# A graph attention layer in split precision: attention by pairs of heads, and low parts of weight slabs on VectorE

## Chip, cores, metric

One core of a Trainium2 chip. The metric is the device time of one execution in microseconds.

## The reference

`x` is 384x1024, H = 16 heads of D = 64, N = 384 nodes, 6528 edges; all weights are 1024x1024, all data float32.

```python
h = maximum(layernorm(x), 0)
q = h @ wq.T + bq;  k = h @ wk.T + bk;  v = h @ wv.T + bv
q2 = (q @ wiq.T + biq);  k2 = (k @ wik.T + bik);  v2 = (v @ wiv.T + biv)   # cut into 16 heads of 64
mask = full((N, N), -inf); mask[src, dst] = softplus(edge_weights)[type - 1]; diagonal filled
scores = q2 @ k2.T / 8 + mask          # per head, 384x384
out = softmax(scores) @ v2             # per head, 384x64
y = x + out @ wo.T + bo
```

## The kernel before

**Split products.** A float32 array is held as a high part rounded to fp32r (`hi`) and the rest (`lo`). A product is three matmuls: hi by hi, lo by hi, hi by lo (`products`, L735, L736, L739). ScalarE writes the high part, VectorE or GpSimd subtracts it from the source.

**Slabs.** The weights come as 56 slabs of 512 KB. SyncE loads slab `s` into `raw` (3 buffers) once the low part of slab `s-3` exists. `split_hi(s)` (ScalarE, L387) fills one of four `w_hi` buffers, `split_lo(s)` fills `w_lo` on VectorE (L629) or GpSimd (L322), as `lo_by_vector` says: before, odd slabs below 16 and all of 16 to 37 by VectorE, the others (0 and the even ones below 16, and 38 to 55) by GpSimd.

**Stages**, each engine running its own instructions in the order written, with waits on semaphores: layernorm and transposes; v (slabs 0 to 7), v2 (8 to 15), q (16 to 23), k (24 to 31); slabs 32 to 47 alternate between q2 and k2, one slab (`tile`, 24 matmuls) for 128 output rows, that is for a pair of heads; slabs 48 to 55 are the output projection (`out_part`, seven pieces, each a sum over 8 row blocks `k`, block `k` being head pair `k`). In the first two stages VectorE also works out each edge's cell (`edge_unit`: four L523, then L532 and L535), and GpSimd scatters the values into `cells` in DRAM (`scatter`); `build_mask` reads them back later. GpSimd adds the bias `bo` to the reloaded x (L367).

**Attention**, loop over heads `i`. A q2/k2 tile is evacuated by `tile_hi_part` and `tile_lo_part` in halves of 64 partitions: for each head, q2 high stands on its own 64 partitions and q2 low on the other 64. `k2_other_half` (VectorE, L617, four copies of 64x384 per pair) puts k2 high and k2 low on both halves. So `scores(i)` needs two matmuls of 128 rows per block of 128 nodes (L850, L852), six per head. Per head then: VectorE adds the mask and takes the row maximum (L688), scales it (L674); ScalarE takes the exponential (L470); VectorE inverts the sum; GpSimd multiplies (L375); one step later TensorE transposes the nine 128x128 blocks (`turn_probs`, L862), ScalarE and VectorE split them (L466, L679), and `heads_values` multiplies by v2 (L877, L878). ScalarE (L482, half of the result plus bias), VectorE (L721) and ScalarE again (L458, `a_hi`), then GpSimd (`a_lo`), put the head's result together. Between the transposes and `heads_values` of a step stands one tile of 24 matmuls, or, in the last steps, part of the output projection.

## Time and profile before

| | us |
|---|---|
| median of 3 runs (lowest, highest) | 330.95 (326.81, 332.99) |
| profiled execution: device time | 330.76 |
| its span, first to last instruction | 329.2 |
| TensorE busy in it | 301.1 (91%) |
| VectorE / ScalarE / GpSimd busy | 221.5 / 163.6 / 169.8 |

The device time holds 1.56 us beside the span. The profile's durations of matmuls overlap, since they are pipelined: the distance between two starts is what one costs. A wait names the instruction whose end released it.

### The profile page before, as it was taken

The page shows a single profiled execution, that of the slowest core. Times are in us where ns is not written, and L with a number is a line of the kernel's source. Part 1 is how long each engine was busy: PE and PEld are TensorE (multiplying, and loading weights), DVE is VectorE, ACT ScalarE, POOL GpSimd, SP SyncE. Part 2 cuts the span into 40 slices and gives each one's busy share as a digit, 9 for nine tenths or more (in the row PEclk, how much of TensorE's full clock was granted, in tenths as well). Part 3 has the DMA queues.
Part 4 walks back from the last instruction along what each step waited for, and adds up shares of the span by engine and source line. Part 5 has one row for each costly group of instructions (what it writes and reads, how often), then busy time and mean ns, then how long its engine had stood idle before and what let it go on. Part 6 is the DMA issues. An engine that isn't in the chain of part 4 may idle for free.

```text
span 329.2 us, 4826 instructions
## 1 busy us (share of the span) xinstructions
PE 301.1 (91%) x1696; PEld 280.2 (85%) x1696; DVE 221.5 (67%) x568; ACT 163.6 (50%) x304; POOL 169.8 (52%) x156
## 2 busy tenths in 40 slices
PE   1879999999999999999969997979797979999996
PEld 0569899788899999999969997979797979878886
DVE  4887986943444444444896979797979796992231
ACT  3663533233433333333445785858586765794300
POOL 5416777765446555555705565655556464456200
PEclk9999999999999999999998999999999998999999
DMA  7816444338733343436332122020212111121031
GB/s 203 343 65 193 126 131 128 130 130 273 286 116 120 126 120 125 129 129 196 127 127 64 67 87 105 10 103 22 85 41 72 58 64 67 64 86 43 2 127 66
DMA packets 13640, 37.48 MB, mean 114 GB/s; under 512 B 3248, under 2 KB 4528, under 8 KB 13616
## 3 DMA queue, kind: packets, MB, share of 16 engines
q1 hardware_dynamic: 11312, 35.93, 32.3%
q0 software_dynamic: 2016, 1.21, 1.5%
q8 instruction: 14, 0.23, 0.3%
q14 instruction: 10, 0.08, 0.1%
q10 hardware_dynamic: 288, 0.03, 0.1%
HBM read 34.38 MB, written 2.78 MB: 113 GB/s over the span
## 4 chain that ended last, share of the span: by engine, by line
PE 62%; DVE 21%; ACT 9%; DMA 3%; issue 3%; SPq 1%; POOL 0%; DVEq 0%
PE bank L735 18%; PE bank L739 18%; PE bank L736 18%; DVE k_lo L617 5%; DVE k_lo L602 3%; ACT prob L470 3%; DVE w_lo L629 3%; PE bank L862 2%; DVE k_hi L617 2%; PE bank L850 2%; ACT pt_hi L466 2%; DMA raw<-in_slabs 2%; DMA x_sb<-in_x 2%; PE bank L852 2%; ACT k_hi L398 1%
## 5 line engine op out<-in xcount | busy, mean ns | idle before, releaser
L349 POOL DMA_INDIRECT cells<-value,cell x51 | 56.0, 1099 | 47.4 <-DMA cells<-value,cell 39.6
L735 PE MATMUL bank<-a_hi,w_hi 128*128 128x384 f32 x192 | 65.3, 340 | 1.5 <-DVE w_lo L629 0.9
L387 ACT ACTIVATE w_hi<-raw 128x1024 fp32r<-128x1024 f32 x51 | 53.5, 1053 | 24.6 <-PE bank L739 18.4
L739 PE MATMUL bank<-a_lo,w_hi 128*128 128x384 f32 x192 | 64.5, 336 | 1.0 <-DVE a_lo L642 1.0
L736 PE MATMUL bank<-a_hi,w_lo 128*128 128x384 f32 x192 | 64.2, 334 | 0.0
L375 POOL TENSOR_SCALAR prob<-prob,row_inv 128x384 f32<-128x384 f32 x42 | 25.8, 628 | 62.4 <-DVE row_inv L703 62.4
L322 POOL TENSOR_TENSOR w_lo<-raw,w_hi 128x1024 fp32r<-128x1024 f32 x21 | 51.0, 2427 | 7.1 <-ACT w_hi L387 6.9
L629 DVE TENSOR_TENSOR w_lo<-raw,w_hi 128x1024 fp32r<-128x1024 f32 x30 | 41.4, 1381 | 15.0 <-ACT w_hi L387 14.5
L735 PEld LDWEIGHTS bank<-a_hi,w_hi 128*128 128x128 f32 x192 | 36.1, 188 | 1.9 <-DVE w_lo L629 1.1
L739 PEld LDWEIGHTS bank<-a_lo,w_hi 128*128 128x128 f32 x192 | 36.0, 188 | 1.7 <-DVE a_lo L642 1.5
L736 PEld LDWEIGHTS bank<-a_hi,w_lo 128*128 128x128 f32 x192 | 36.1, 188 | 0.0
L466 ACT ACTIVATE pt_hi<-bank 128x384 fp32r<-128x384 f32 x48 | 20.1, 488 | 23.4 <-PE bank L862 23.3
L470 ACT ACTIVATE prob<-prob,neg_max 128x384 f32<-128x384 f32 x48 | 29.1, 615 | 5.2 <-DVE neg_max L674 5.2
L850 PE MATMUL bank<-k_hi,q 128*128 128x384 f32 x48 | 18.2, 378 | 13.5 <-DVE k_lo L617 13.5
L679 DVE TENSOR_TENSOR pt_lo<-bank,pt_hi 128x384 fp32r<-128x384 f32 x48 | 23.7, 549 | 3.9 <-ACT pt_hi L466 3.8
L393 ACT ACTIVATE b_hi<-bank,bias 128x384 fp32r<-128x384 f32 x16 | 9.3, 581 | 34.0 <-PE bank L739 34.0
L688 DVE CUSTOM_DVE_ANT_0 prob<-bank,work 128x384 f32<-128x384 f32 x48 | 25.1, 548 | 0.3
L592 DVE SCALAR_TENSOR_TENSOR b_lo<-bank,bias,b_hi 128x384 fp32r<-128x384 f32 x16 | 9.9, 616 | 21.1 <-ACT b_hi L393 21.0
L850 PEld LDWEIGHTS bank<-k_hi,q 128*128 128x128 f32 x48 | 9.7, 203 | 16.1 <-DVE k_lo L617 16.1
L735 PE MATMUL bank<-b_hi,w_hi 128*128 128x384 f32 x64 | 22.0, 343 | 0.5 <-DVE q L602 0.5
L735 PE MATMUL bank<-c_hi,w_hi 128*128 128x384 f32 x64 | 22.3, 349 | 0.0
L736 PE MATMUL bank<-c_hi,w_lo 128*128 128x384 f32 x64 | 21.7, 339 | 0.0
(131 smaller groups left out, 694.9 us busy)
## 6 DMA issues: line engine op xcount, KB each, us to landing
raw<-in_slabs SPq DMA_DIRECT2D x56, 512.0 KB
x_sb<-in_x SPq DMA_DIRECT2D x5, 512.0 KB, 6.1
out_y<-x_sb SPq DMA_DIRECT2D x5, 256.0 KB, 2.2
cells<-prob SPq DMA_DIRECT2D x2, 576.0 KB, 9.7
cells<-value,cell POOLq DMA_INDIRECT x51
work<-cells POOLq DMA_DIRECT2D x1, 576.0 KB, 4.9
prob<-cells POOLq DMA_DIRECT2D x1, 576.0 KB, 6.5
x_sb<-in_x SPq DMA_DIRECT2D x2, 256.0 KB, 3.2
```

The source lines that it names most:

```text
L322: nc.gpsimd.tensor_tensor(lo, raw[:, s % RAW, :], hi.bitcast(F32), ALU.subtract).then_inc(slab_lo, 1)
L349: nc.gpsimd.indirect_dma_start(out=cells[c][:, :], out_offset=bass.IndirectOffsetOnAxis(ap=cell[:, t:t + 1], axis=0), in_=value[:, t:t + 1 ...
L375: nc.gpsimd.tensor_scalar(prob[:, i % 2, t, :], prob[:, i % 2, t, :], row_inv[:, i % 2, t:t + 1], 1.0, ALU.mult, ALU.mult).then_inc(prob_o ...
L387: nc.scalar.activation(split_place(s)[0], raw[:, s % RAW, :], ACT.Copy).then_inc(slab_hi, 1)
L466: nc.scalar.activation(pt_hi[:, m, :], pt_bank[m][:, 0:N], ACT.Copy).then_inc(pt_hi_ok, 1)
L470: nc.scalar.activation(prob[:, i % 2, t, :], prob[:, i % 2, t, :], ACT.Exp, scale=SCALE, bias=neg_max[:, i % 2, t:t + 1], accum_out=row_su ...
L629: nc.vector.tensor_tensor(lo, raw[:, s % RAW, :], hi.bitcast(F32), ALU.subtract).then_inc(slab_lo_dve, 1)
L688: nc.vector.tensor_tensor_reduce(out=prob[:, i % 2, t, :], in0=score_bank[t][:, 0:N], in1=mask[:, t, :], scale=1.0, scalar=-3.4e38, op0=AL ...
L735: nc.tensor.matmul(psum, w[0], a[0], start=first, stop=False)
L736: nc.tensor.matmul(psum, w[1], a[0], start=False, stop=False)
L739: return nc.tensor.matmul(psum, w[0], a[1], start=False, stop=last)
L850: nc.tensor.matmul(score_bank[n][:, 0:N], q2[:, turn, h % 2, m], k2_hi[:, turn, h % 2, :], start=True, stop=False)
```

## The change

The attention loop runs over pairs of heads `j`. q2 and k2 are kept as plain high and low parts of 128 partitions, head `2j` on the first 64 and `2j+1` on the last; `k2_other_half` is gone, and each tile is evacuated by one instruction on each engine in place of two. `scores(j, n)` gives block `n` of both heads by three matmuls each of 64 rows, taken from the two heads in turn and written to two PSUM banks. Four banks serve scores and two the transposes. VectorE takes the minimum of the negated scores, which is the bias of the exponential, so L674 goes. In a step the work of pair `j` (scores, maximum, exponential) is interleaved with the transposes and values of both heads of pair `j-1`, and the slab tiles are cut in two halves of 12 matmuls (`filler`); the output projection is spread over the last three steps in another order, and at the end all seven pieces are closed by their last block in turn. VectorE adds `bo` to x during pair 0, where GpSimd did it before. VectorE makes the low parts of slabs 1 to 37. GpSimd keeps slab 0 and slabs 38 to 55, and the multiplications of all blocks.

TensorE where the scores of a new pair begin, before (`q2` and `k2_hi`, `k2_lo` are the operands, bank 0 to 2 the scores, bank 5 the transposed probabilities):

```order
L850 MATMUL bank0<-k2_hi,q2 128x384 [waits masked,tile_lo]
L852 MATMUL bank0<-k2_lo,q2 128x384
L850 MATMUL bank1<-k2_hi,q2 128x384 [waits masked]
L852 MATMUL bank1<-k2_lo,q2 128x384
L850 MATMUL bank2<-k2_hi,q2 128x384 [waits masked]
L852 MATMUL bank2<-k2_lo,q2 128x384
L862 MATMUL bank5<-ident,prob 128x128 [waits pt_lo_ok,prob_ok]
L862 MATMUL bank5<-ident,prob 128x128 x2
```

and now:

```order
L880 MATMUL bank0<-k2_hi,q2_hi 128x384 [waits masked,tile_lo]
L880 MATMUL bank1<-k2_hi,q2_hi 128x384
L880 MATMUL bank0<-k2_lo,q2_hi 128x384
L880 MATMUL bank1<-k2_lo,q2_hi 128x384
L880 MATMUL bank0<-k2_hi,q2_lo 128x384
L880 MATMUL bank1<-k2_hi,q2_lo 128x384
L880 MATMUL bank2<-k2_hi,q2_hi 128x384
L880 MATMUL bank7<-k2_hi,q2_hi 128x384
L880 MATMUL bank2<-k2_lo,q2_hi 128x384
L880 MATMUL bank7<-k2_lo,q2_hi 128x384
L880 MATMUL bank2<-k2_hi,q2_lo 128x384
L880 MATMUL bank7<-k2_hi,q2_lo 128x384
```

The scores of the pair's first two blocks are twelve 64-row matmuls, in twos on the two halves of the partitions, with the wait at the first; the transposes follow behind these.

VectorE between the first head's and the second head's work, before, from the split of the transposed probabilities on:

```order
L679 TENSOR_TENSOR pt_lo<-bank,pt_hi 128x384 [waits pt_hi_ok] x3
L703 RECIPROCAL row_inv<-row_sum 128x1 [waits exp_done] x3
L617 CAST k_hi<-k_hi 64x384 [waits k2_read,k2_step]
L617 CAST k_hi<-k_hi 64x384
L617 CAST k_lo<-k_lo 64x384 x2
L602 SCALAR_TENSOR_TENSOR q<-bank,bias,q 64x384 [waits tile_hi] x2
L721 TENSOR_TENSOR work<-bank,work 64x384 [waits head_lo,half_ok]
```

and now, over the start of a pair:

```order
L695 TENSOR_TENSOR pt_lo<-bank,pt_hi 128x384 [waits pt_hi_ok] x2
L691 RECIPROCAL row_inv<-row_sum 128x1 [waits exp_done] x2
L695 TENSOR_TENSOR pt_lo<-bank,pt_hi 128x384 [waits pt_hi_ok]
L618 SCALAR_TENSOR_TENSOR q_lo<-bank,bias,q_hi 128x384 [waits tile_hi]
L681 ISA prob,neg_max<-bank,work 128x384 [waits score_done]
L681 ISA neg_max 128x1
L681 ISA work,neg_max<-bank,work 128x384 [waits score_done]
L681 ISA neg_max 128x1
L704 TENSOR_TENSOR work<-bank,work 64x384 [waits head_lo,half_ok]
```

The four copies in front of the next scores are gone, and the result of the last head stands between the two parts of the maximum.

VectorE in the first step of attention, before, with the maximum of head 0:

```order
L688 ISA prob,row_max<-bank,work 128x384 [waits mask_ok,score_done]
L688 ISA row_max 128x1
L688 ISA prob,row_max<-bank,work 128x384 [waits mask_ok,score_done]
L688 ISA row_max 128x1
L674 TENSOR_SCALAR neg_max<-row_max 128x1 [waits masked]
L688 ISA prob,row_max<-bank,work 128x384 [waits mask_ok,score_done]
L688 ISA row_max 128x1
L674 TENSOR_SCALAR neg_max<-row_max 128x1 [waits masked] x2
L703 RECIPROCAL row_inv<-row_sum 128x1 [waits exp_done] x3
```

and now, from the fourth block of the maximum of pair 0:

```order
L681 ISA prob,neg_max<-bank,work 128x384 [waits score_done]
L681 ISA neg_max 128x1
L710 TENSOR_TENSOR x_sb<-x_sb,work 128x1024 [waits y_in]
L691 RECIPROCAL row_inv<-row_sum 128x1 [waits exp_done] x2
L710 TENSOR_TENSOR x_sb<-x_sb,work 128x1024 [waits y_in]
L691 RECIPROCAL row_inv<-row_sum 128x1 [waits exp_done] x2
L710 TENSOR_TENSOR x_sb<-x_sb,work 128x1024 [waits y_in]
L618 SCALAR_TENSOR_TENSOR k_lo<-bank,bias,k_hi 128x384 [waits tile_hi]
```

The additions of `bo` stand between the maxima and the inversions.

```diff
-        q2 = sb("q2", [P, 2, 2, N], F32R)
-        k2_hi = sb("k2_hi", [P, 2, 2, N], F32R)
-        k2_lo = sb("k2_lo", [P, 2, 2, N], F32R)
+        q2_hi = sb("q2_hi", [P, 2, N], F32R)
+        q2_lo = sb("q2_lo", [P, 2, N], F32R)
+        k2_hi = sb("k2_hi", [P, 2, N], F32R)
+        k2_lo = sb("k2_lo", [P, 2, N], F32R)
         work = sb("work", [P, NT * N + N], F32)
-        prob = sb("prob", [P, 2, NT, N], F32)
+        prob = sb("prob", [P, 3, NT, N], F32)
...
+        probs = [[prob[:, 0], prob[:, 1]],
+                 [prob[:, 2], work2[:, 0:NT * N].rearrange("p (t n) -> p t n", n=N)]]
...
-        score_bank = bank[0:3]
-        pt_bank = bank[5:8]
+        score_bank = [bank[0], bank[1], bank[2], bank[7]]
+        pt_bank = bank[5:7]
...
-            return s % 2 == 1 if s < LO_SHARED else s < LO_ALL
+            return 1 <= s < LO_ALL
...
+        def slabs_of_step(j):
+            return [range(38 + 2 * j, 39 + 2 * j), range(39 + 2 * j, 40 + 2 * j)] if j < PAIRS - 2 else [
+                range(50 + 3 * (j - 6), 51 + 3 * (j - 6)), range(51 + 3 * (j - 6), 53 + 3 * (j - 6))]
...
-            for s in range(2, LO_SHARED, 2):
-                split_lo(s)
...
-            pool.wait_ge(y_in, 16 * (NT + 1))
-            for t in range(NT):
-                nc.gpsimd.tensor_tensor(y[:, t, :], y[:, t, :], bo_sb, ALU.add).then_inc(y_ok, 1)
...
+            def norm_part(j, n):
+                for x in range(2):
+                    c = 2 * n + x
+                    pool.wait_ge(inv_ok, chunk_at(j, n, x) + 1)
+                    nc.gpsimd.tensor_scalar(probs[j % 2][x][:, n, :], probs[j % 2][x][:, n, :],
+                                            row_inv[:, j % 2, c:c + 1], 1.0, ALU.mult, ALU.mult).then_inc(prob_ok, 1)
+            for j in range(PAIRS):
+                first, second = slabs_of_step(j)
+                norm_part(j, 0)
+                norm_part(j, 1)
+                if j >= 2:
+                    pair_lo_part(j - 2)
+                for s in first:
+                    split_lo(s)
+                norm_part(j, 2)
+                for s in second:
                     split_lo(s)
...
+            for j in range(PAIRS + 1):
+                first, second = slabs_of_step(j) if j < PAIRS else ((), ())
+                h = 2 * (j - 1)
+                if j >= 2:
+                    half_part(h - 1)
+                if j < PAIRS:
+                    exp_part(j, 0)
+                if j >= 2:
+                    pair_hi_part(j - 2)
+                if j >= 1:
+                    pt_hi_part(h, 0)
+                    pt_hi_part(h, 1)
+                if j < PAIRS:
+                    exp_part(j, 1)
+                for s in first:
                     split_hi(s)
...
+                if j >= 1:
+                    pt_hi_part(h, 2)
+                if j < PAIRS - 1:
+                    tile_hi_part(3 * KT + 3 + 2 * j)
+                if j < PAIRS:
+                    exp_part(j, 2)
+                if j >= 1:
+                    half_part(h)
+                    pt_hi_part(h + 1, 0)
+                    pt_hi_part(h + 1, 1)
+                for s in second:
+                    split_hi(s)
+                if j >= 1:
+                    pt_hi_part(h + 1, 2)
+                if j < PAIRS - 2:
+                    tile_hi_part(3 * KT + 4 + 2 * j)
+            half_part(H - 1)
...
-            def k2_other_half(pair):
...
-            split_lo(1)
+            for s in range(1, AHEAD):
+                split_lo(s)
...
-                    if s == QK0 + 1:
-                        k2_other_half(0)
...
+            def max_part(j, n):
+                for x in range(2):
+                    c, at = 2 * n + x, chunk_at(j, n, x)
+                    dve.wait_ge(score_done, at + 1)
+                    if at == 0:
+                        dve.wait_ge(mask_ok, 1)
+                    if at == 6:
+                        dve.wait_ge(y_ok, NT)
+                    nc.vector.tensor_tensor_reduce(
+                        out=probs[j % 2][x][:, n, :], in0=score_bank[c % 4][:, 0:N], in1=mask[:, n, :], scale=-SCALE,
+                        scalar=3.4e38, op0=ALU.add, op1=ALU.min,
+                        accum_out=neg_max[:, j % 2, c:c + 1]).then_inc(masked, 1)
...
+            def y_part(t):
+                dve.wait_ge(y_in, 16 * (NT + 1))
+                nc.vector.tensor_tensor(y[:, t, :], y[:, t, :], bo_sb, ALU.add).then_inc(y_ok, 1)
+            for j in range(PAIRS + 1):
+                h = 2 * (j - 1)
+                if j < PAIRS:
+                    max_part(j, 0)
+                if j >= 2:
+                    head_part(h - 1)
+                if j < PAIRS:
+                    max_part(j, 1)
+                    if j == 0:
+                        y_part(0)
+                    inv_part(j, 0)
+                    if j == 0:
+                        y_part(1)
+                if j == PAIRS:
                     pair_lo_part(PAIRS - 2)
...
+                if j >= 1:
+                    pt_lo_part(h, 0)
+                    pt_lo_part(h, 1)
+                if j < PAIRS:
+                    inv_part(j, 1)
+                    if j == 0:
+                        y_part(2)
+                if j >= 1:
+                    pt_lo_part(h, 2)
+                if j < PAIRS - 1:
+                    tile_lo_part(3 * KT + 3 + 2 * j)
+                if j < PAIRS:
+                    max_part(j, 2)
+                if j >= 1:
+                    head_part(h)
+                    pt_lo_part(h + 1, 0)
+                    pt_lo_part(h + 1, 1)
+                if j < PAIRS:
+                    inv_part(j, 2)
+                if j >= 1:
+                    pt_lo_part(h + 1, 2)
+                if j < PAIRS - 2:
+                    tile_lo_part(3 * KT + 4 + 2 * j)
+            head_part(H - 1)
...
-            def scores(h):
-                turn = h // 2 % 2
-                if h % 2 == 0:
-                    pe.wait_ge(tile_lo, 3 * KT + h + 2)
+                    tile(t, c_hi, c_lo, ks)
+            def scores(j, n):
+                turn, m = j % 2, slice(n * P, (n + 1) * P)
+                if n == 0:
+                    pe.wait_ge(tile_lo, 3 * KT + 2 * j + 2)
+                for x in range(2):
+                    at = chunk_at(j, n, x)
+                    if n == 0 and j >= 1:
+                        pe.wait_ge(masked, at - 1)
+                    elif n == NT - 1:
+                        pe.wait_ge(masked, at - 3)
+                for p, (q, k) in enumerate(((q2_hi, k2_hi), (q2_hi, k2_lo), (q2_lo, k2_hi))):
+                    for x in range(2):
+                        own, _ = rows_of(x)
+                        mm = nc.tensor.matmul(score_bank[(2 * n + x) % 4][:, 0:N], q[own, turn, m], k[own, turn, :],
+                                              start=(p == 0), stop=(p == 2))
+                        if p == 2:
+                            mm.then_inc(score_done, 1)
+            def turn_probs(h, m):
+                i = h * NT + m
+                if m == 0:
+                    pe.wait_ge(prob_ok, chunk_at(h // 2, NT - 1, h % 2) + 1)
+                if i >= 2:
+                    pe.wait_ge(pt_lo_ok, i - 1)
                 for n in range(NT):
-                    if h >= 1:
-                        pe.wait_ge(masked, (h - 1) * NT + n + 1)
-                    m = slice(n * P, (n + 1) * P)
-                    nc.tensor.matmul(score_bank[n][:, 0:N], q2[:, turn, h % 2, m], k2_hi[:, turn, h % 2, :],
-                                     start=True, stop=False)
-                    nc.tensor.matmul(score_bank[n][:, 0:N], q2[:, turn, h % 2, m], k2_lo[:, turn, h % 2, :],
-                                     start=False, stop=True).then_inc(score_done, 1)
-            def turn_probs(h):
-                pe.wait_ge(prob_ok, (h + 1) * NT)
-                for m in range(NT):
-                    if h >= 1:
-                        pe.wait_ge(pt_lo_ok, (h - 1) * NT + m + 1)
-                    for n in range(NT):
-                        mm = nc.tensor.transpose(pt_bank[m][:, n * P:(n + 1) * P],
-                                                 prob[:, h % 2, n, m * P:(m + 1) * P], ident[:])
-                    mm.then_inc(pt_done, 1)
+                    mm = nc.tensor.transpose(pt_bank[i % 2][:, n * P:(n + 1) * P],
+                                             probs[h // 2 % 2][h % 2][:, n, m * P:(m + 1) * P], ident[:])
+                mm.then_inc(pt_done, 1)
...
+            halves = (range(0, KT // 2), range(KT // 2, KT))
+            def filler(j, at):
+                if j < PAIRS - 1 and at < 2:
+                    pair_tile(3 * KT + 3 + 2 * j, halves[at])
+                elif j < PAIRS - 2:
+                    pair_tile(3 * KT + 4 + 2 * j, halves[at - 2])
+                elif j == PAIRS - 2:
+                    if at == 2:
+                        pe.wait_ge(tile_lo, 5 * KT)
+                    out_part(0, range(2 * (at - 2), 2 * (at - 2) + 2))
+                elif j == PAIRS - 1:
+                    if at == 0:
+                        out_part(0, range(4, 5))
+                    elif at == 1:
+                        pe.wait_ge(masked, chunk_at(j, 1, 0) + 1)
+                        out_part(1, range(0, 5))
+                    elif at == 2:
+                        out_part(0, range(5, 6))
+                        pe.wait_ge(masked, chunk_at(j, 2, 0) + 1)
+                        out_part(2, range(0, 3))
+                    else:
+                        out_part(2, range(3, 6))
+                        out_part(1, range(5, 6))
+                elif at == 0:
+                    out_part(3, range(0, 3))
+                elif at == 1:
+                    out_part(3, range(3, 6))
+                elif at == 2:
+                    out_part(4, range(0, 4))
                 else:
+                    out_part(4, range(4, 6))
                     for n in range(NT):
                         out_part(n, [KT - 2])
...
-                    heads_values(i - 1)
-            out_part(NT, range(0, KT - 1))
-            for n in range(NT):
-                out_part(n, [KT - 1])
-            out_part(NT, [KT - 1])
-            out_part(NT + 1, range(KT))
-            out_part(NT + 2, range(KT))
-            out_part(NT + 3, range(KT))
+            for j in range(PAIRS + 1):
+                h = 2 * (j - 1)
+                if j < PAIRS:
+                    scores(j, 0)
+                    scores(j, 1)
+                if j >= 1:
+                    turn_probs(h, 0)
+                    turn_probs(h, 1)
+                filler(j, 0)
+                if j >= 1:
+                    turn_probs(h, 2)
+                filler(j, 1)
+                if j < PAIRS:
+                    scores(j, 2)
+                if j >= 1:
+                    heads_values(h)
+                    turn_probs(h + 1, 0)
+                    turn_probs(h + 1, 1)
+                filler(j, 2)
+                if j >= 1:
+                    turn_probs(h + 1, 2)
+                filler(j, 3)
+                if j >= 1:
+                    heads_values(h + 1)
+            for piece in (3, 4):
+                out_part(piece, [KT - 2])
+            out_part(NT + 2, range(0, KT - 1))
+            out_part(NT + 3, range(0, KT - 1))
+            for piece in range(len(out_pieces)):
+                out_part(piece, [KT - 1])
```

## Rows read from the trace of the kernel before

**Rows 1.** The page: the chain that ended last, by line.

```profile
PE bank L735 18%; PE bank L739 18%; PE bank L736 18%; DVE k_lo L617 5%; DVE k_lo L602 3%; ACT prob L470 3%; DVE w_lo L629 3%; PE bank L862 2%; DVE k_hi L617 2%; PE bank L850 2%; ACT pt_hi L466 2%; DMA raw<-in_slabs 2%; DMA x_sb<-in_x 2%; PE bank L852 2%; ACT k_hi L398 1%
```

**Rows 2.** Waits of TensorE: who for whom, total, times, longest.

```profile
PE bank L850 <- DVE k_lo L617: 13.5, 8, 2.3
```

**Rows 3.** Windows: stretch, length, busy PE, PEld, DVE, ACT, POOL, clock, DMA.

```profile
171.84:186.10 14.26, 14.26 (x75) 13.96 (x75) 11.11 (x36) 9.05 (x21) 6.07 (x7) 0.88 0.22 74
237.16:254.04 16.88, 14.77 (x91) 14.38 (x91) 14.41 (x41) 11.90 (x27) 9.44 (x9) 1.00 0.18 62
270.90:286.10 15.20, 14.92 (x78) 13.97 (x78) 11.80 (x38) 10.46 (x25) 5.19 (x5) 0.89 0.22 71
```

**Rows 4.** Timeline, VectorE and GpSimd between two pairs of heads.

```profile
234.03 3.08 DVE L617 CAST k_lo<-k_lo 64x384 fp32r<-64x384 f32 x2
...
234.44 2.45 POOL L322 TENSOR_TENSOR w_lo<-raw,w_hi 128x1024 fp32r<-128x1024 f32 x1
```

**Rows 5.** Timeline of TensorE after that: start, duration.

```profile
237.16 0.44 PE L850 MATMUL bank<-k_hi,q 128*128 128x384 f32 x1 [2.12 <-DVE k_lo L617]
...
238.32 1.14 PE L862 MATMUL bank<-ident,prob 128*128 128x128 f32 x9
239.22 0.42 PE L735 MATMUL bank<-c_hi,w_hi 128*128 128x384 f32 x1
239.48 0.34 PE L736 MATMUL bank<-c_hi,w_lo 128*128 128x384 f32 x1
...
243.32 0.33 PE L739 MATMUL bank<-c_lo,w_hi 128*128 128x384 f32 x1
```

**Rows 6.** Timeline around the start of attention, three engines.

```profile
155.53 7.10 POOL L367 TENSOR_TENSOR x_sb<-x_sb,work 128x1024 f32<-128x1024 f32 x3
...
157.96 5.76 DVE L629 TENSOR_TENSOR w_lo<-raw,w_hi 128x1024 fp32r<-128x1024 f32 x1 [0.33 <-ACT w_hi L387]
...
165.15 0.41 PE L735 MATMUL bank<-b_hi,w_hi 128*128 128x384 f32 x1 [0.46 <-DVE q L602]
...
171.84 0.66 PE L850 MATMUL bank<-k_hi,q 128*128 128x384 f32 x1 [2.29 <-DVE k_lo L617]
...
175.17 0.41 PE L736 MATMUL bank<-c_hi,w_lo 128*128 128x384 f32 x1
```

**Rows 7.** Timeline of the value projection, tiles 3 and 4.

```profile
33.13 3.03 DVE L532 SCALAR_TENSOR_TENSOR live<-later,key_dump 128x4 f32<-128x4 f32 x1
...
33.71 2.42 POOL L322 TENSOR_TENSOR w_lo<-raw,w_hi 128x1024 fp32r<-128x1024 f32 x1
...
38.23 0.41 PE L735 MATMUL bank<-a_hi,w_hi 128*128 128x384 f32 x1 [0.53 <-DVE b_lo L592]
```

**Rows 8.** The page: groups of instructions, busy, mean ns of one.

```profile
L375 POOL TENSOR_SCALAR prob<-prob,row_inv 128x384 f32<-128x384 f32 x42 | 25.8, 628 | 62.4 <-DVE row_inv L703 62.4
L322 POOL TENSOR_TENSOR w_lo<-raw,w_hi 128x1024 fp32r<-128x1024 f32 x21 | 51.0, 2427 | 7.1 <-ACT w_hi L387 6.9
...
L466 ACT ACTIVATE pt_hi<-bank 128x384 fp32r<-128x384 f32 x48 | 20.1, 488 | 23.4 <-PE bank L862 23.3
L470 ACT ACTIVATE prob<-prob,neg_max 128x384 f32<-128x384 f32 x48 | 29.1, 615 | 5.2 <-DVE neg_max L674 5.2
...
L679 DVE TENSOR_TENSOR pt_lo<-bank,pt_hi 128x384 fp32r<-128x384 f32 x48 | 23.7, 549 | 3.9 <-ACT pt_hi L466 3.8
...
L688 DVE CUSTOM_DVE_ANT_0 prob<-bank,work 128x384 f32<-128x384 f32 x48 | 25.1, 548 | 0.3
```

**Rows 9.** Timeline of TensorE, the last output pieces.

```profile
320.09 0.39 PE L739 MATMUL bank<-c_lo,a_hi 128*128 128x512 f32 x1
320.32 0.28 PE L735 MATMUL bank<-b_hi,a_hi 128*128 128x256 f32 x1
...
325.95 0.28 PE L739 MATMUL bank<-c_lo,a_hi 128*128 128x256 f32 x1
```

**Rows 10.** The page: issues of the output's DMA.

```profile
out_y<-x_sb SPq DMA_DIRECT2D x5, 256.0 KB, 2.2
```

214 lines of the change are left out of this document (54 added, 160 removed).

## The prediction

> **What bounds the kernel now.** I read the chain that ended last first. Matmuls of the slab tiles (L735, L736, L739) carry 54% of it, and the next names are VectorE's low parts and copies of k2, L617 and L602 [rows 1]. So the end is set by TensorE, and by what it waits for. The waits of TensorE say for what: 13.5 us in eight waits of the scores for L617 [rows 2]. The windows give the loop: a pair of heads takes 16.88 us, in which the other engines have room [rows 3].
>
> Then the cost of each kind of TensorE work, by distances between starts [rows 5]. A tile's 2nd matmul starts at 239.48 and its 24th at 243.32: 0.174 us each. Nine transposes go from 238.32 to 239.22, 0.10 each. The first matmul behind them takes 0.26 to the next start, 0.09 more than usual. A pair is 48 tile matmuls (8.35), 12 of scores (2.09), 12 of values (2.09), 18 transposes with two such seams (1.98): 14.5 us. The other 2.4 us of the 16.88 is the wait of 2.12 and its restart.
>
> The wait has a cause of its own: the two copies of k2 low take 3.08 us, beside GpSimd's slab subtraction from 234.44 to 236.89 [rows 4]. The same picture stands twice elsewhere. A subtraction on four elements takes VectorE 3.03 us while GpSimd subtracts a slab from 33.71 to 36.13 [rows 7]. One slab's low part takes 5.76 us from 157.96, and GpSimd's additions of `bo` end at 162.63, 1.1 us before it [rows 6]. VectorE's instructions with all operands in SBUF stand still while GpSimd works; by the last case such a low part costs 1.1 us when alone.
>
> **The sum, against the profiled execution** (span 329.2, device time 330.76, 0.19 below the median; I add the 1.56 us beside the span at the end).
>
> *Low parts of slabs 2 to 14 to VectorE.* TensorE's only wait here that they can touch is 0.53 us at 38.23, for a tile's low part that stood behind the 3.03 us [rows 7]. Per two tiles (8.4 us) VectorE takes on 1.1 us and loses a block of up to 3.0, so I count the wait and its restart as gone: -0.6. If VectorE were late by all it takes on, it would be +7.7 (7 x 1.1). Edge cells come up to 1.1 us later each; GpSimd, rid of seven times 2.43 us [rows 8], scatters earlier, behind the matmuls of five stages: the mask is read only at the entry into attention. SyncE, which loads slab s after the low part of s-3, gets the even ones sooner: nothing.
>
> *Entry into attention.* Without GpSimd's additions the 5.76 us become 1.1, and without `k2_other_half(0)` the scores follow the tile from 165.15 at once: it starts 0.55 earlier (0.46 and restart) and ends 24 x 0.174 = 4.2 later, at 169.3 by the old clock of the trace, against scores at 171.84 [rows 6]. That is -3.1.
>
> *Clock.* After that wait the granted clock is at the 1.2 GHz level: ten starts take 3.33 us (171.84 to 175.17) instead of 1.74, 1.6 lost [rows 6]; the window's mean is 0.88, and the window from 270.90 has 0.89, the same loss again [rows 3]. Both follow an idle TensorE of over 2 us; none that long is left: -3.2. The other waits of about 2.1 us kept 2.4 GHz (1.00 in the window of 237.16), so a return of the drop is possible without a warning.
>
> *The copies.* Seven waits besides the first hold 13.5 - 2.3 = 11.2 us; with restarts (2.4 for 2.12) 12.7: -12.7. The halved evacuations, L674 and the copies leave VectorE with slack in every step; worth nothing by itself.
>
> *Scores.* 96 matmuls of 128 rows (16.7 us) become 144 of 64 rows. No row shows a 64-row matmul. Upper bound: each costs 0.174, whatever its rows, 25.1 us. Lower bound: two on different halves of the partitions and in different banks cost as one, 72 x 0.174 = 12.5. Each still loads its own 128 columns of weights, and transposes, which also load for each matmul, come every 0.10 [rows 5]; two loads are 0.20. I take 72 x 0.20 = 14.4, because that row holds the nearest limit if the halves work side by side: -2.3. (By the Trainium skill, TensorE: Matmul & The Clock Gate, Part 3, small matmuls at different row positions run at once, a pack costing one duration and some 4 ns for each more; the sum would then be 1.6 us lower than mine. No row here shows it.)
>
> *Seams.* Transposes come in four groups per pair instead of two (16 more seams in all) and scores in two groups with a seam at either end (32): 48 x 0.09 = +4.3 [rows 5]. Bounds for the 32: nothing, or a drained array. A matmul lasts 0.33 and its successor starts after 0.17; waiting for its end and restarting (0.44 against 0.33 for the first after a wait) is 0.16 + 0.11 = 0.27, which makes +5.8 more.
>
> *New waits.* In a step, the transposes of block 2 wait for the low part of block 0, as two banks serve them. By [rows 5, 8], from the first score matmul: scores of block 0 are out at 0.9 with what lies between engines; two maxima to 2.0 (0.55 each); two exponentials to 2.7 (0.6); `a_hi` 3.2; `pt_hi` of block 0 3.7; VectorE, after head result, maxima and inversions at 3.8, has `pt_lo` at 4.3. TensorE is there at 4.1 (scores 1.3, six transposes 0.7, half a tile 2.1). For the second head the same walk gives 11.7 against 11.5. I take 0.5 a step, steps 1 to 5: 2.5. Steps 6 to 8 have shorter fillers, of 512-column matmuls at 0.23 [rows 9]: step 7 starts with three of them (0.7 instead of 2.1), +1.6; step 6, +1.2; step 8, +0.5. Entry of step 1: VectorE's three additions (1.1 each) meet GpSimd's multiplications (0.63) and its slab of 2.43 [rows 8] and wait for them; the maximum of block 2 ends near 10.0, GpSimd then has slab 38 in front, and the multiplied block comes 1.4 after TensorE wants it. Together +7.2; bounds nothing and twice that. Behind TensorE's waiting transposes stands the whole rest of its queue, and GpSimd's, VectorE's and ScalarE's next steps with it.
>
> *Tail.* Last start 325.95, span's end 3.25 us later. Now seven pieces close within 4 us and VectorE and the output DMA (2.2 us a piece [rows 10]) follow in a row: +1.2, between 0 and 3. The matmuls are the same.
>
> Sum: -0.6 - 3.1 - 3.2 - 12.7 - 2.3 + 4.3 + 7.2 + 1.2 = **-9.2**, a span of 320.0 and **321.6 us**.
>
> **Rivals.** (1) *The halves take turns* (slower). Place: L880. Each 64-row matmul costs what a 128-row one does, 0.174: +10.7, 332.3 us, above before. It decides from 0.32 us for two, (330.95 - 321.6)/72 above my 0.20. For it: all TensorE rows show one matmul after another. Against it: they all use all rows. Chance 0.10; with (2) also true, 338, chance 0.02.
>
> (2) *Each change between 128-row and 64-row work drains the array*: 32 x 0.27 instead of 0.09, 327.4 us, chance 0.15. The seam of 0.09 behind the transposes, also a change of kind, speaks against it, no row on a change of rows for it. The Trainium skill, TensorEngine Tiling (Array Packing), Key Properties, has this rule: changing the tiling mode drains TensorE.
>
> (3) *The chain over three engines takes the wait's place*: ScalarE does its exponentials before `pt_hi`, so if each step's two waits come to 1.7 instead of 0.5, all eight steps give 9.6: 331 us. For it: my margins are 0.2 us. Against: the walk counts whole durations, and instructions on one engine follow each other a little faster. Chance 0.08.
>
> (4) *Seams of scores cost nothing and the new waits half*: -2.9 - 3.6, 315.1 us. Chance 0.17. That the copies' wait stays is out: nothing copies any more.
>
> **How the numbers follow.** The forecast, with its own range 318 to 325.5, has 0.48. The range for 8 in 10 reaches from (4)'s 315, with 0.5 for error, to 330.5, with (2) and the lower half of (3) in it: 314.5 to 330.5. Outside lie (1) and a part of (3) and (4). 2% is about what a measurement of this kernel can tell: 324.3 and 337.6. Faster: (4) 0.17, of the forecast 0.43, of (2) and (3) 0.04, 0.64. Slower: 0.03. The same: 0.33.
>
> **What the changed profile would show.** No L617. TensorE's start of scores at about 168.2, and 1.00 clock there. L880 in twos with 0.20 between the twos; 0.174 between single ones is rival 1. The first matmul behind scores 0.26 to its successor; 0.44 is rival 2. A pair at 15.3 us; waits of the transposes for `pt_lo` of 0.2 to 0.3 each, over 0.8 is rival 3. VectorE's L710 longer than 1.1 us beside L369. No wait near 38 us. Wrong I would be most through L880, or a wait that I did not walk to, above all in steps 6 to 8 and in the slabs of the output projection, whose low parts GpSimd still makes.

## The result, and the profile after

| | before | after |
|---|---|---|
| median (lowest, highest), us | 330.73 (326.81, 332.99), 4 runs | 318.87 (318.79, 318.88), 4 runs |
| ratio, 95% interval | | 0.9677 [0.9634, 0.972] |
| profiled span | 329.2 | 317.3 |
| granted clock, mean | 0.989 | 1.00 |

The change makes the kernel 3.2% faster; 321.6 us was forecast, and the range of 314.5 to 330.5 holds the result. Some executions of the kernel before and of three experiments, all with GpSimd making low parts of the first slabs, took 5 us or more longer than the rest, for a reason that isn't shown: the ratios leave them out, the medians given below don't.

The changed kernel's page, busy times, the clock in 40 slices, and the chain that ended last by line, to be read against [rows 1]:

```profile
PE 299.7 (94%) x1744; PEld 270.1 (85%) x1744; DVE 179.1 (56%) x476; ACT 154.7 (49%) x288; POOL 147.0 (46%) x152
...
PEclk9999999999999999999999999999999999999999
...
PE bank L767 23%; PE bank L763 22%; PE bank L764 22%; PE bank L893 4%; PE bank L880 3%; DMA x_sb<-in_x 2%; PE bank L908 2%; ACT prob L461 2%; PE bank L909 2%; DVE work L704 1%; DVE pt_lo L695 1%; ACT work L475 1%; DVE prob L681 1%; DVE x_sb L755 1%; ACT k_hi L395 1%
```

The matmuls of slab tiles (now L763, L764, L767) rose from 54% of the chain to 67%. VectorE's copies are gone from it, its evacuations of k2 are no longer among the lines named, and VectorE is busy 42 us less. The waits of TensorE, in place of [rows 2]:

```profile
PE bank L893 <- DVE pt_lo L695: 2.6, 4, 1.4
```

The windows of the eight steps, from one first score matmul to the next, in the columns of [rows 3]:

```profile
168.21:178.93 10.72, 10.72 (x69) 9.71 (x68) 8.25 (x23) 6.89 (x16) 6.16 (x5) 1.00 0.14 45
178.93:194.22 15.29, 15.14 (x97) 13.52 (x96) 8.63 (x28) 10.43 (x24) 11.55 (x12) 1.00 0.32 104
...
224.82:240.13 15.31, 15.16 (x97) 13.52 (x96) 8.94 (x29) 10.83 (x25) 9.10 (x10) 1.00 0.21 69
...
255.44:270.32 14.88, 14.01 (x86) 11.51 (x85) 8.61 (x28) 11.18 (x25) 8.67 (x10) 1.00 0.22 73
270.32:287.88 17.56, 16.20 (x91) 13.20 (x91) 7.79 (x26) 10.60 (x24) 13.21 (x12) 1.00 0.18 61
```

Scores start at 168.21 in place of 171.84, a pair takes 15.3 us in place of 16.88, and no window is under 1.00. The timeline of TensorE at one start of a step, to be read against [rows 5] (a row joins instructions of one form; x2 are the two heads):

```profile
224.82 0.44 PE L880 MATMUL bank<-k_hi,q_hi 64*128 64x384 f32 x2
225.11 0.34 PE L880 MATMUL bank<-k_lo,q_hi 64*128 64x384 f32 x2
225.28 0.34 PE L880 MATMUL bank<-k_hi,q_lo 64*128 64x384 f32 x2
...
225.80 0.36 PE L880 MATMUL bank<-k_hi,q_lo 64*128 64x384 f32 x2
226.09 0.88 PE L893 MATMUL bank<-ident,prob 128*128 128x128 f32 x6
226.72 0.42 PE L763 MATMUL bank<-c_hi,w_hi 128*128 128x384 f32 x1
...
228.72 0.34 PE L767 MATMUL bank<-c_lo,w_hi 128*128 128x384 f32 x1
229.01 0.55 PE L893 MATMUL bank<-ident,prob 128*128 128x128 f32 x3
229.31 0.42 PE L763 MATMUL bank<-c_hi,w_hi 128*128 128x384 f32 x1
...
231.31 0.34 PE L767 MATMUL bank<-c_lo,w_hi 128*128 128x384 f32 x1
231.58 0.44 PE L880 MATMUL bank<-k_hi,q_hi 64*128 64x384 f32 x2
231.86 0.34 PE L880 MATMUL bank<-k_lo,q_hi 64*128 64x384 f32 x2
232.03 0.34 PE L880 MATMUL bank<-k_hi,q_lo 64*128 64x384 f32 x2
232.30 0.44 PE L908 MATMUL bank<-pt_hi,v 128*128 128x384 f32 x1
232.58 0.34 PE L909 MATMUL bank<-pt_lo,v 128*128 128x384 f32 x1
...
236.02 0.34 PE L767 MATMUL bank<-b_lo,w_hi 128*128 128x384 f32 x1
236.51 0.55 PE L893 MATMUL bank<-ident,work 128*128 128x128 f32 x3 [0.15 <-DVE pt_lo L695]
236.81 0.42 PE L763 MATMUL bank<-b_hi,w_hi 128*128 128x384 f32 x1
```

Three things are to be seen. Two 64-row matmuls take 0.17 together, what one of 128 rows takes. A change of rows lengthens two distances, the one across it and the next: around the scores of block 2 they are 0.27 and 0.28 (231.31 to 231.86) going in and 0.27 and 0.28 (232.03 to 232.58) going out, where 0.17 would be usual, so some 0.2 in all for each change. And the transposes of block 2 come 0.29 and 0.49 behind a tile's last matmul: short waits, of which only one carries a mark. The long ones are in steps 6 to 8:

```profile
267.11 0.55 PE L893 MATMUL bank<-ident,work 128*128 128x128 f32 x3 [0.84 <-DVE pt_lo L695]
...
274.51 0.55 PE L893 MATMUL bank<-ident,prob 128*128 128x128 f32 x3 [1.36 <-DVE pt_lo L695]
...
291.04 0.55 PE L893 MATMUL bank<-ident,prob 128*128 128x128 f32 x3 [0.27 <-DVE pt_lo L695]
```

### The profile page after: what moved, and what is told of

It is laid out like the page before. It is cut to its first block, busy times and chain, and to the rows that moved or that the text cites. A ratio compares the mean times of both kernels' runs of the same rounds, so it can differ in the third digit from the quotient of the medians.

```text
span 317.3 us, 4822 instructions
## 1 busy us (share of the span) xinstructions
PE 299.7 (94%) x1744; PEld 270.1 (85%) x1744; DVE 179.1 (56%) x476; ACT 154.7 (49%) x288; POOL 147.0 (46%) x152
## 4 chain that ended last, share of the span: by engine, by line
PE 79%; DVE 9%; ACT 5%; issue 3%; DMA 2%; SPq 1%; POOL 0%; DVEq 0%; ACTq 0%
PE bank L767 23%; PE bank L763 22%; PE bank L764 22%; PE bank L893 4%; PE bank L880 3%; DMA x_sb<-in_x 2%; PE bank L908 2%; ACT prob L461 2%; PE bank L909 2%; DVE work L704 1%; DVE pt_lo L695 1%; ACT work L475 1%; DVE prob L681 1%; DVE x_sb L755 1%; ACT k_hi L395 1%
## 5 line engine op out<-in xcount | busy, mean ns | idle before, releaser
L763 PE MATMUL bank<-a_hi,w_hi 128*128 128x384 f32 x192 | 65.3, 340 | 0.9 <-DVE w_lo L630 0.9
L767 PE MATMUL bank<-a_lo,w_hi 128*128 128x384 f32 x192 | 64.5, 336 | 1.1 <-DVE a_lo L643 1.0
L764 PE MATMUL bank<-a_hi,w_lo 128*128 128x384 f32 x192 | 64.2, 334 | 0.0
L630 DVE TENSOR_TENSOR w_lo<-raw,w_hi 128x1024 fp32r<-128x1024 f32 x37 | 45.3, 1225 | 18.3 <-ACT w_hi L390 16.2
L369 POOL TENSOR_SCALAR prob<-prob,row_inv 128x384 f32<-128x384 f32 x36 | 22.6, 637 | 69.5 <-DVE row_inv L691 69.5
L767 PEld LDWEIGHTS bank<-a_lo,w_hi 128*128 128x128 f32 x192 | 36.0, 188 | 1.8 <-DVE a_lo L643 1.7
L763 PEld LDWEIGHTS bank<-a_hi,w_hi 128*128 128x128 f32 x192 | 36.1, 188 | 1.4 <-DVE w_lo L630 1.1
L764 PEld LDWEIGHTS bank<-a_hi,w_lo 128*128 128x128 f32 x192 | 36.1, 188 | 0.0
L695 DVE TENSOR_TENSOR pt_lo<-bank,pt_hi 128x384 fp32r<-128x384 f32 x48 | 25.2, 552 | 17.0 <-ACT pt_hi L468 17.0
L325 POOL TENSOR_TENSOR w_lo<-raw,w_hi 128x1024 fp32r<-128x1024 f32 x14 | 33.5, 2392 | 0.0
L461 ACT ACTIVATE prob<-prob,neg_max 128x384 f32<-128x384 f32 x36 | 21.9, 610 | 18.7 <-DVE neg_max L681 18.7
L468 ACT ACTIVATE pt_hi<-bank 128x384 fp32r<-128x384 f32 x48 | 21.5, 482 | 3.5 <-PE bank L893 3.3
L763 PE MATMUL bank<-c_hi,w_hi 128*128 128x384 f32 x64 | 22.5, 352 | 0.0
L681 DVE CUSTOM_DVE_ANT_0 prob<-bank,work 128x384 f32<-128x384 f32 x36 | 18.9, 553 | 6.2 <-PE bank L880 6.0
L763 PE MATMUL bank<-b_hi,w_hi 128*128 128x384 f32 x64 | 22.4, 350 | 0.0
L767 PE MATMUL bank<-b_lo,w_hi 128*128 128x384 f32 x64 | 21.5, 336 | 0.0
L767 PE MATMUL bank<-c_lo,w_hi 128*128 128x384 f32 x64 | 21.5, 336 | 0.0
L764 PE MATMUL bank<-c_hi,w_lo 128*128 128x384 f32 x64 | 21.4, 335 | 0.0
```

The source lines that it names most:

```text
L325: nc.gpsimd.tensor_tensor(lo, raw[:, s % RAW, :], hi.bitcast(F32), ALU.subtract).then_inc(slab_lo, 1)
L369: nc.gpsimd.tensor_scalar(probs[j % 2][x][:, n, :], probs[j % 2][x][:, n, :], row_inv[:, j % 2, c:c + 1], 1.0, ALU.mult, ALU.mult).then_in ...
L461: nc.scalar.activation(probs[j % 2][x][:, n, :], probs[j % 2][x][:, n, :], ACT.Exp, scale=-1.0, bias=neg_max[:, j % 2, c:c + 1], accum_out ...
L468: nc.scalar.activation(pt_hi[:, m, :], pt_bank[(h * NT + m) % 2][:, 0:N], ACT.Copy).then_inc(pt_hi_ok, 1)
L630: nc.vector.tensor_tensor(lo, raw[:, s % RAW, :], hi.bitcast(F32), ALU.subtract).then_inc(slab_lo_dve, 1)
L681: nc.vector.tensor_tensor_reduce(out=probs[j % 2][x][:, n, :], in0=score_bank[c % 4][:, 0:N], in1=mask[:, n, :], scale=-SCALE, scalar=3.4e ...
```

## The experiments

Lines of code in them are those of the kernel that they change.

### Do the halves of the array work side by side?

First, one head's three matmuls ahead of the other's:

```diff
-                for p, (q, k) in enumerate(((q2_hi, k2_hi), (q2_hi, k2_lo), (q2_lo, k2_hi))):
-                    for x in range(2):
+                for x in range(2):
+                    for p, (q, k) in enumerate(((q2_hi, k2_hi), (q2_hi, k2_lo), (q2_lo, k2_hi))):
```

> The changed kernel, with one difference: in each block the three score matmuls of one head come first and those of the other head after them, in place of turns. The count, the shapes, the banks and the seams to 128-row work stay. Theory (two 64-row matmuls cost as one because they stand on different halves of the partitions and overlap): within a head they can't, so 144 matmuls cost up to 0.174 each, 25.1 us in place of the 12.5 that the changed kernel shows; about +12 us, less at most 2.6 for waits on the low parts of the probabilities that this hides: 328 to 332 us, and distances of 0.17 within a head. Rival (a 64-row matmul costs half of a 128-row one by itself, in any order): 318.9 us as now, distances of 0.087.

Measured: 318.97 us (318.76 to 319.24), the changed kernel's 318.87. The first theory forecast 328 to 332 and fell, as it was put; but its timeline does not speak for the rival either:

```profile
224.99 0.45 PE L879 MATMUL bank<-k_hi,q_hi 64*128 64x384 f32 x2
225.27 0.34 PE L879 MATMUL bank<-k_lo,q_hi 64*128 64x384 f32 x2
```

In the program a hi-hi matmul (high part of q2, high part of k2) of head 0 is followed by two more of head 0, and only then comes the second head's hi-hi. In the trace the hi-hi of both heads come together, x2 at 224.99, then both hi-lo. The second head's matmul started beside one that stands three places ahead of it. So the order didn't test what I meant it to: the halves do not wait for each other in program order, over three instructions at least. The next run puts both heads on one half:

```diff
-                        own, _ = rows_of(x)
+                        own, _ = rows_of(0)
```

> The changed kernel, with the score matmuls of both heads on the first 64 partitions (the second head's scores are left out, the first head's are made twice). Count, shape, banks, order and seams stay. The run with one head's three matmuls ahead of the other's cost the same as the changed kernel, and its trace had the twos as before, the matmuls of the second head starting beside those of the first although they stand behind them in the program: so either each half of the array runs its own queue, or a 64-row matmul is cheap by itself. First theory (own queues): on one half nothing runs side by side, 72 more distances of 0.17, +12.5 less up to 2.6 of hidden waits: 329 to 331.5 us, L880 singly every 0.17. Rival (half the rows, half the price): 318.9 us, as now.

Measured: 327.03 us (326.86 to 327.13), span 325.3, 8.0 more than the changed kernel's.

```profile
229.09 0.61 PE L880 MATMUL bank<-k_hi,q_hi 64*128 64x384 f32 x2
229.55 0.51 PE L880 MATMUL bank<-k_lo,q_hi 64*128 64x384 f32 x2
229.90 0.50 PE L880 MATMUL bank<-k_hi,q_lo 64*128 64x384 f32 x2
230.24 0.51 PE L880 MATMUL bank<-k_hi,q_hi 64*128 64x384 f32 x2
```

Twos now come every 0.35, one matmul every 0.17. A 64-row matmul is not cheap by itself; the two halves work side by side, which this shows. That it costs 8.0 and not 12.5 has its reason in the same trace: from step to step it takes 16.31 in place of 15.31, though the scores of a pair take 1.54 more (2.29 against 1.27 up to the transposes, 1.24 against 0.72 for block 2). The other 0.54 are waits for `pt_lo` that are gone: its block-2 transposes follow 0.18 behind the tile, not 0.29 and 0.49, and each group of three takes 0.24, not 0.30. So the changed kernel waits about 0.5 us in each ordinary step.

### What does a change of rows cost?

```diff
                 if j < PAIRS:
                     scores(j, 0)
-                    scores(j, 1)
                 if j >= 1:
                     turn_probs(h, 0)
+                if j < PAIRS:
+                    scores(j, 1)
+                if j >= 1:
                     turn_probs(h, 1)
```

> The changed kernel, with the transposes of block 0 put between the scores of block 0 and those of block 1, in steps 1 to 7: 14 more changes between 64-row and 128-row work, nothing else more. Theory (a change costs about 0.2 us, as the distances 0.26 to 0.29 beside the usual 0.10 and 0.17 show): +2.9, about 321.8 us. Rival a (a change costs what I forecast, 0.09): +1.3, 320.2. Rival b (the array is drained and restarted, 0.27 each): +3.8, 322.7. Since block 0 is transposed 0.8 us earlier, up to 1 us of the waits in steps 6 to 8 may go as well, if they hang on the transposes; I think they hang on ScalarE, which is late there, and stay.

Measured: 320.23 us (320.09 to 320.45), +1.4.

```profile
225.61 0.44 PE L880 MATMUL bank<-k_hi,q_hi 64*128 64x384 f32 x2
...
227.84 0.42 PE L763 MATMUL bank<-c_hi,w_hi 128*128 128x384 f32 x1
...
229.85 0.34 PE L767 MATMUL bank<-c_lo,w_hi 128*128 128x384 f32 x1
230.03 0.49 PE L893 MATMUL bank<-ident,prob 128*128 128x128 f32 x3
```

From the first score matmul to the first tile matmul it takes 2.23 (225.61 to 227.84) where the changed kernel takes 1.90 (224.82 to 226.72): 0.33 for two changes, 0.17 each, in which the six transposes are also cut into two groups of three. For 14 changes that would be 2.3. The missing part is waits without a mark that got shorter: block 2's transposes now stand 0.18 behind the tile and not 0.29, and take 0.24 and not 0.30. So an ordinary step grows by 0.17 only, and the marked waits of TensorE for `pt_lo` gave back 0.4 (2.2 against 2.6). With the 0.2 that the distances in the changed kernel show, a change costs 0.17 to 0.2: neither my 0.09 nor the 0.27 of a drained array.

### Where the gain is: the copies of k2

```diff
-                        last = nc.vector.tensor_copy(part[other, turn, h, :], part[own, turn, h, :].bitcast(F32))
+                        c = slice(0, N) if pair < 2 else slice(0, 1)
+                        last = nc.vector.tensor_copy(part[other, turn, h, c], part[own, turn, h, c].bitcast(F32))
```

> The kernel before; its copies of k2 to the other half of the partitions move one column in place of 384 for pairs 2 to 7 (the copying of the other columns is left out, so scores of these pairs use wrong values there). Theory (the copies' wait of about 1.9 us a pair, with 0.25 for the restart, and the second drop of the clock carry the gain of the change): six waits of 11.2/7 = 1.6 with 0.2 of restart each, -10.8, and the clock's -1.6: about 318 us, that is all the gain of the whole change, though the score matmuls keep their 128 rows. Rival (behind the copies stand other things just as late, VectorE's evacuation of the k2 tile above all): -5 or less, 326 or more.

Measured: 316.49 us (314.16 to 323.26), ratio 0.9597 [0.9419, 0.9774]; the profiled span is 312.9 at clock 1.00. The kernel before has 326.0 at that clock (329.2 less two drops of 1.6), 13.1 more. But 1.8 of this lie ahead of the first scores (170.09 against 171.84 in [rows 6]), where this edit changes nothing:

```profile
152.09 7.12 POOL L367 TENSOR_TENSOR x_sb<-x_sb,work 128x1024 f32<-128x1024 f32 x3
...
153.85 6.46 DVE L630 TENSOR_TENSOR w_lo<-raw,w_hi 128x1024 fp32r<-128x1024 f32 x1 [0.33 <-ACT w_hi L387]
...
170.09 0.45 PE L851 MATMUL bank<-k_hi,q 128*128 128x384 f32 x1 [0.54 <-DVE k_lo L618]
```

GpSimd's additions of `bo` started 3.4 us earlier here than in the profiled execution of the kernel before, and met the slab ahead of the one that they met there. The instructions up to this point are the same in both kernels, so this isn't the edit's work; I take it for the chance of an execution, of which no second trace was taken. The copies' time is worth the other 11.3. Without it the old loop is 4.4 us shorter in span than the changed kernel. So the rest of the new loop costs, and the question is why the copies were late. In the kernel before the two copies of k2 high take 1.12 and the two of k2 low 3.08 [rows 4]; VectorE stands still beside GpSimd.

```profile
232.90 1.12 DVE L617 CAST k_hi<-k_hi 64x384 fp32r<-64x384 f32 x2
```

If that is the cause, it is enough to move them to a place where GpSimd is idle:

```diff
+                if i % 2 == 1 and i < H - TILES_AHEAD:
+                    k2_other_half((i + 1) // 2)
                 if i == H - TILES_AHEAD:
                     k2_other_half(PAIRS - 1)
                 if i < H:
                     for t in range(NT):
                         dve.wait_ge(exp_done, i * NT + t + 1)
                         nc.vector.reciprocal(row_inv[:, i % 2, t:t + 1], row_sum[:, i % 2, t:t + 1]).then_inc(inv_ok, 1)
...
-                if i % 2 == 1 and i < H - TILES_AHEAD:
-                    k2_other_half((i + 1) // 2)
```

> The kernel before, with VectorE's four copies of k2 for the next pair placed ahead of the three inversions of the odd head in place of behind them; nothing else. There GpSimd has nothing to do, because its multiplications wait for the inversions. Theory (the copies are late because GpSimd's slab subtraction holds VectorE off, 3.08 us for two, and not because of their number): the copies take 1.6 to 2.2 us in all in place of 4.2 and end about 3 us earlier, the waits of 1.9 us for pairs 1 to 7 go and with them all drops of the clock but the first: -13 to -14, 316 to 318 us, as good as the changed kernel or better, with scores of 128 rows. Rival (the inversions, 1.6 to 2.2 us later, delay GpSimd's multiplications and the transposes behind them): the wait moves to the transposes, 322 to 329 us.

Measured: 316.56 us (314.74 to 324.96), ratio 0.9523 [0.9411, 0.9635], span 313.7 at clock 1.00. Its timeline of VectorE and GpSimd:

```profile
237.32 1.03 POOL L326 TENSOR_TENSOR a_lo<-work,a_hi 128x384 fp32r<-128x384 f32 x1 [0.60 <-ACT a_hi L458]
...
239.91 0.72 DVE L617 CAST k_hi<-k_hi 64x384 fp32r<-64x384 f32 x2
240.65 0.72 DVE L617 CAST k_lo<-k_lo 64x384 fp32r<-64x384 f32 x2
241.40 0.28 DVE L705 RECIPROCAL row_inv<-row_sum 128x1 f32<-128x1 f32 x3
...
241.67 1.72 POOL L375 TENSOR_SCALAR prob<-prob,row_inv 128x384 f32<-128x384 f32 x3 [3.32 <-DVE row_inv L705]
```

The same four copies take 1.44 us, 0.36 each, less even than expected, because GpSimd does nothing from 238.35 to 241.67. Counted from the head's result ahead of them (L721, at 228.63 before and at 236.12 here) they end 3.2 us earlier: 2.8 of it is their shorter time, 0.5 their earlier place. The waits of TensorE for L617 are 1.0 in three, where [rows 2] has 13.5 in eight. One wait of 0.7 for GpSimd's multiplications is all that came in their place in the attention. The scores start at 170.04 here, again with the same code ahead of them as before, so of the 12.3 us between the two spans at equal clock (326.0 to 313.7) 10.5 are the edit's. So it was the meeting with GpSimd, not the number of copies.

### The low parts alone

```diff
-            return s % 2 == 1 if s < LO_SHARED else s < LO_ALL
+            return 1 <= s < LO_ALL
```

With it go GpSimd's and VectorE's calls of `split_lo`, as in the change.

> The kernel before, with VectorE making the low parts of slabs 1 to 37, and nothing else of the change. Theory (the block of VectorE behind GpSimd's slab subtraction is gone, TensorE waited for it 0.53 us at one place): -0.6, about 330.1 us. Rival (VectorE, with 1.1 us more every second slab, comes late): up to +7.7, with waits of TensorE for the low parts of slabs or tiles below 130 us of the span. Second rival: the edge cells come later by so much that the scattering of the mask reaches the entry into attention: +1 or more, seen as a wait for the mask there.

Measured: 327.78 us (325.57 to 329.12, 10 runs), ratio 0.995 [0.9906, 0.9994]. The profiled span is 324.0 at clock 1.00. The wait near 38 us is gone, as forecast, but the span gained more: its scores start at 168.72, not at 171.84. GpSimd's timeline says why:

```profile
142.41 7.10 POOL L362 TENSOR_TENSOR x_sb<-x_sb,work 128x1024 f32<-128x1024 f32 x3
```

These are its additions of `bo`, 13.1 us earlier than in [rows 6], far more than the 3.4 by which one execution differed from another. Rid of seven slabs it scatters earlier and comes to them earlier, so they don't meet VectorE's last slab ahead of the attention: that takes 1.23 there, not 5.76.

The ten runs also show the clock, because this kernel sits on its edge. Spans by granted clock:

| granted clock | spans, us |
|---|---|
| 1.00 | 324.0, 324.3, 324.3 |
| 0.994, 0.995 | 325.6, 325.8, 326.3 |
| 0.989 | 327.1, 327.1, 327.4, 327.6 |

Each 0.005 of the mean is one drop, of about 1.6 us. So with the same waits of about 2 us in it, this kernel has none, one or two drops from one execution to the next. The kernel before spreads wider still (326.81 to 332.99), and the changed one, with no wait over 1.4 in the attention, has no drop (318.79 to 318.88).

### The low parts shared again, and the bias on either engine

In the changed kernel, the low parts of even slabs below 16 go back to GpSimd:

```diff
-            return 1 <= s < LO_ALL
+            return s % 2 == 1 if s < Q0 else s < LO_ALL
```

> The changed kernel with its second part undone: GpSimd makes the low parts of the even slabs 2 to 14 again. Theory: the wait near 38 us is back, +0.6, about 319.5 us; the attention is not touched. Rival: nothing measurable, 318.9, if the wait of 0.5 is taken up again by a later one; second rival: the shorter work of VectorE lets something else start earlier, below 318.5.

Measured: 318.80 and 319.62 us in the two executions that the ratio counts, 0.9626 [0.9558, 0.9693]; the median of all six is 324.92, the highest 326.60. The profiled run is the one of 318.80, with a span of 317.3, the changed kernel's. So `lo_by_vector`'s new rule is worth between nothing and 0.8 us on top of the rest of the change; VectorE's 3.06 us beside GpSimd's slab are back at 32.52, and TensorE doesn't wait there.

In the changed kernel, `y_part` goes and GpSimd has its loop back:

```diff
+            pool.wait_ge(y_in, 16 * (NT + 1))
+            for t in range(NT):
+                nc.gpsimd.tensor_tensor(y[:, t, :], y[:, t, :], bo_sb, ALU.add).then_inc(y_ok, 1)
```

> The changed kernel with the bias added to x by GpSimd ahead of the attention, as before, and not by VectorE in pair 0. Theory (VectorE's slab subtraction next to the attention takes 5.8 us in place of 1.2 beside GpSimd's additions, and the last tiles wait for it): the entry comes 0.5 to 3 us later, and if TensorE then idles over 2 us the clock drops as it did before, 1.6 more: 319.4 to 323.5 us, with the scores of the first pair starting later than 168.7. Rival (without the copies of k2 the low part of that slab is early enough in any case): 318.9 or less, because VectorE's three additions, and GpSimd's multiplications that stand still beside them, are gone from pair 0.

Measured: 319.02 us (318.59 to 319.55); scores start at 168.07. The theory falls. GpSimd's three additions take from 142.31 to 149.42, again ahead of the place in question, and what they meet is another slab of VectorE:

```profile
140.62 1.23 DVE L634 TENSOR_TENSOR w_lo<-raw,w_hi 128x1024 fp32r<-128x1024 f32 x1 [0.33 <-ACT w_hi L394]
144.78 5.73 DVE L634 TENSOR_TENSOR w_lo<-raw,w_hi 128x1024 fp32r<-128x1024 f32 x1 [0.33 <-ACT w_hi L394]
```

The same 5.7 us as at the entry, but here the slab is not due yet, and nobody waits.

In the kernel before, that loop goes, and VectorE has in its first three heads:

```diff
+                if i < 3:
+                    dve.wait_ge(y_in, 16 * (NT + 1))
+                    nc.vector.tensor_tensor(y[:, i, :], y[:, i, :], bo_sb, ALU.add).then_inc(y_ok, 1)
```

> The kernel before, with the bias added to x by VectorE during the first three heads in place of GpSimd ahead of them, and nothing else of the change. Theory: the slab subtraction of 5.76 us becomes 1.2, the tile behind it starts up to 0.5 us earlier, and the copies of k2 for the first pair, which also ran late, come earlier; whether the clock's first drop goes hangs on whether the wait at the first scores, 2.3 us, shrinks below 2: -0.5 to -3.0, 328 to 330.3 us. Rival: the additions of VectorE fall beside GpSimd's multiplications and slab subtraction in the first heads and cost there what they save: no change.

Measured: 332.37 us (329.09 to 333.24), ratio 1.0007 [0.9949, 1.0065], no change. The slab ahead of the attention takes 1.22 (157.98) and the wait of the first scores falls from 2.29 to 0.40, both as expected, and the next pair gives it back, as its copies stand behind the second addition of `bo` and take 4.35 beside GpSimd (182.22 to 186.59):

```profile
169.26 0.45 PE L850 MATMUL bank<-k_hi,q 128*128 128x384 f32 x1 [0.40 <-DVE k_lo L614]
...
186.64 0.69 PE L850 MATMUL bank<-k_hi,q 128*128 128x384 f32 x1 [3.52 <-DVE k_lo L614]
```

The rival had it: the additions cost later on VectorE what they save ahead. In the changed kernel this edit pays no more than here, as the run before this one shows; it only does no harm.

### The order in the last steps

In steps 6 to 8 ScalarE and VectorE split the transposed probabilities ahead of the exponentials, head results and inversions. The core of it, on ScalarE:

```diff
-                if j < PAIRS:
+                if j < PAIRS - 2:
                     exp_part(j, 0)
...
                     pt_hi_part(h, 1)
+                if j >= PAIRS - 2:
+                    if j < PAIRS:
+                        exp_part(j, 0)
+                    pair_hi_part(j - 2)
```

> The changed kernel with another order of ScalarE and VectorE in the last three steps: the high and low parts of the transposed probabilities come ahead of the exponentials, of the head's result and of the inversions, and the last slab's high part of a step behind them. Theory (the four waits of TensorE for pt_lo, 1.36, 0.84, 0.27 and 0.15 us, 2.6 in all, come from ScalarE's order and not from the transposes): steps 6 to 8 lose their waits, with restarts of 0.1 each -2.8, about 316.1 us; the step of 15.3 us is not touched. Rival (the exponentials, now later, delay GpSimd's multiplications and so the next step's transposes): the waits move to the start of the next step, 318.9 or more.

Measured: 317.44 us (317.18 to 317.67), span 315.8, 1.5 less than the changed kernel. The four marked waits are gone, and two others came:

```profile
269.08 0.44 PE L930 MATMUL bank<-pt_hi,v 128*128 128x384 f32 x1 [0.69 <-DVE pt_lo L707]
273.78 0.50 PE L785 MATMUL bank<-w_hi,a_hi 128*128 128x512 f32 x1 [0.64 <-DVE neg_max L693]
```

So the waits came from the order on ScalarE and VectorE, as the theory said; about half of the 2.8 us expected was lost to what now stood later.

### A version that beats both

The kernel before with early copies, and VectorE making the low parts of slabs 1 to 37:

> The same as the run with early copies, and VectorE makes the low parts of slabs 1 to 37 as in the changed kernel. Theory: the two add up, since they stand in different stages; with the low parts alone the profiled span was 324.0 at a granted clock of 1.00, against 326.0 for the kernel before with its two drops of 1.6 taken off, -2.0: 314 to 316 us, below both kernels. Rival (the first stages' gain is taken up by the wait of the first pair for its copies): 316 to 318, as with early copies alone.

Measured: **314.06 us** (313.79 to 314.71, 4 runs), ratio to before 0.9469 [0.9394, 0.9544]; 1.5% below the changed kernel. Its span is 312.6 at clock 1.00, and its scores start at 168.99. The waits of its TensorE for the copies, and then the timeline at two starts of a pair:

```profile
PE bank L846 <- DVE k_lo L612: 0.9, 3, 0.4
```

```profile
212.23 0.33 PE L846 MATMUL bank<-k_hi,q 128*128 128x384 f32 x1
...
226.78 0.33 PE L846 MATMUL bank<-k_hi,q 128*128 128x384 f32 x1
```

A pair takes 14.55 us. That is the 14.5 that the prediction counted as the work of a pair without the wait, and 0.75 less than in the changed kernel, which saves 0.5 at the scores and pays 0.5 of waits, four changes of rows and two more groups of transposes for it.

## Why the prediction came out as it did

The forecast was the likeliest case; none of the rivals came, though a change of rows cost 0.2, between the 0.09 of the forecast and the 0.27 of rival 2. By its steps, on the span (-9.2 forecast, -11.9 measured):

- *Low parts*, -0.6: the wait near 38 us went, but the step missed the larger effect. "GpSimd, rid of seven times 2.43 us, scatters earlier" stood there, and I stopped at the mask. I didn't follow GpSimd's queue on to the additions of `bo`, which this moves by 13 us.
- *Entry into attention*, -3.1: the scores start 3.6 earlier, which is this term and the 0.5 of the one before, right in size. That a meeting of VectorE's slab with GpSimd's additions made the entry late is borne out, but the cure as I put it, "without GpSimd's additions", isn't needed: with them still on GpSimd the entry is as early (168.07). Either edit alone cures it (168.72 and 169.26); the low parts are enough. And 1.8 of the 3.6 is what the profiled execution of the kernel before was later than others with the same code up to there (170.09 and 170.04 in two runs), which I took for a fixed cost.
- *Clock*, -3.2: right for the execution that it was read from; two drops of 1.6, shown by the spans at each level of the clock.
- *The copies*, -12.7: right within about 1 us. The run with one column shows 11.3, and has a wait of 1.2 for its full copies of pair 1 where the kernel before has 0.39. The runs add what the sum left out, that the gain needed none of the new loop.
- *Scores*, -2.3: the mechanism was right, shown by both heads on one half. The term was mis-sized: twos cost 0.174, the lower bound, not the 0.20 that I took from the transposes; 72 x 0.174 = 12.5, -4.2. Here the rule of the Trainium skill, TensorE: Matmul & The Clock Gate, Part 3, was the better price, and the trace agrees: the twos cost what one 128-row matmul does. And the transposes, from which my 0.20 came, are themselves at 0.08 in groups of three (0.24 from 234.20 to 234.44 in the run on one half), for 16 groups some -1.0 in all, which I didn't forecast.
- *Seams*, +4.3: mis-sized the other way. 32 changes at 0.17 to 0.2, with 16 seams of 0.09, make +6.9 to +7.8. The seam behind transposes was the wrong row to take a change of rows from. The rule of the Trainium skill, TensorEngine Tiling (Array Packing), Key Properties, that a change of mode drains the array, points the right way; the price is below the 0.27 that I made of it. That cancels what the scores gave: nine twos and four changes of a pair come to some 2.3 us, against 2.09 before.
- *New waits*, +7.2: about +6. In steps 1 to 5 the 0.5 each is right (0.54). In steps 6 to 8 the waits of 0.84, 1.36, 0.27 and smaller ones make some 3. The 1.4 at the entry of step 1 did not come: VectorE's additions took 1.2, 1.2 and 1.5, not blocked; it was GpSimd that stood, its four multiplications taking 4.17 in place of 2.3, and it was just in time.
- *Tail*, +1.2: +0.8 (last start 313.26, span's end 317.3).

With 0.2 for a change, at which the parts of an ordinary step add up to its 15.3, these are -3.6 - 3.2 - 12.7 - 4.2 - 1.0 + 7.8 + 6 + 0.8 = -10.1. The other 1.8 us stay open. Some 0.5 of them is a wait of the old kernel that had no term: in its last steps nine transposes take 1.39 (292.43 to 293.82, with a marked wait of 0.24 for VectorE's `row_max`) in place of 0.90. My total was off by 2.7, of which the entry of step 1 and this rest are the most. It came that close in part by luck: scores and transposes were 2.9 too dear and seams 3.5 too cheap, and these errors cancelled each other.

## What to carry to other kernels

Before a loop is rebuilt to get rid of a late instruction, see what stands beside it on the neighbouring engine and try it in the nearest gap of that engine: two moved lines gave 10.5 us here at equal clock (12.3 between the spans of 326.0 and 313.7, less 1.8 at the entry, ahead of the moved lines), the whole change 8.7. Before a difference of two spans is put down to an edit, see whether they already differ ahead of the first instruction that it touches. When work is taken off an engine, follow everything behind it in its queue, to the next stage and further, since it all moves forward and meets other work. And a loop with waits of about 2 us on TensorE is slower by more than the waits, and unsteady, because the clock may fall at each.

## What the hardware showed

- Two 64-row matmuls on different halves start together though one stands three places behind in the program (x2 at 224.99), and cost 0.17 for both; on one half 0.17 each.
- A change between 128-row and 64-row matmuls costs 0.17 to 0.2 us, about 0.1 in each of two distances (0.27 and 0.28 in place of 0.17, 231.31 to 231.86).
- VectorE and GpSimd hold each other off when their operands are in SBUF. A copy of 64x384 takes VectorE 0.36 us alone (239.91 in the run with early copies) and 1.54, the mean of [rows 4], beside a slab subtraction of GpSimd; a slab's low part 1.2 alone and 5.7 to 6.7 beside GpSimd's additions. It goes the other way too: four multiplications of GpSimd took 4.17 us beside VectorE's three additions, and take 2.27 where those are on GpSimd.
- An instruction of VectorE that is held off waits through several of GpSimd's in a row. The low part of a slab ends 1.1 us, its own time, behind the last of the three additions: at 163.72 against 162.63 [rows 6], at 160.31 against 159.21 in the run with one column, at 150.51 against 149.42 with the bias on GpSimd.
